# Attention scores from 32-bit two-part splits in 48 and 50 rows, two heads in the two row halves of the array, in place of bf16 splits in 112 and 115 rows

## The reference

```python
x = x + attn_a(layernorm(x))      # wide heads: 32 query heads, 8 key/value heads, head size 16
x = x + scale * (layernorm(x) @ (2 * w_ffn - 1))
x = x + attn_b(layernorm(x))
x = x + scale * (layernorm(x) @ (2 * w_ffn - 1))

# attention: q, k, v = x @ w_qkv; rope on q and k; four query heads share one key/value head
scores = einsum('bhsd,bhtd->bhst', q, k) / 4
probs = softmax(where(causal, scores, -inf))
out = einsum('bhst,bhtd->bhsd', probs, v) @ w_o
```

## Time and profile before

| | |
|---|---|
| median of three runs | 1555.02 us |
| span of the profiled execution | 1552.2 us, mean granted clock 0.979 |
| PE busy | 1439.5 us, 93% (10,756 matmuls) |
| PE weight loads busy | 799.7 us, 52% |
| DVE busy | 1132.0 us, 73% |
| ACT busy | 998.2 us, 64% |
| POOL busy | 413.6 us, 27% |
| chain that ended last | PE 73%, DVE 11%, issue 8%, POOL 3%, ACT 3%, DMA 1% |

### The profile page before, as it was taken

One profiled execution on the slowest core, in us unless ns is written; L12 is line 12 of the kernel. 1 busy time (PEld: TensorE's weight loads), 2 busy tenths in 40 slices (PEclk: granted clock), 3 DMA queues, 4 the chain that ended last, 5 costly groups with the idle time before them and its releaser, 6 DMA issues.

```text
span 1552.2 us, 36760 instructions
## 1 busy us (share of the span) xinstructions
PE 1439.5 (93%) x10756; PEld 799.7 (52%) x10756; DVE 1132.0 (73%) x1620; ACT 998.2 (64%) x1800; POOL 413.6 (27%) x786
## 2 busy tenths in 40 slices
PE   5989999998798999999879899999988899999997
PEld 4844444446674444444667444444466744444455
DVE  6897777736788777773768877777377887777646
ACT  4967667663496667675349667766625966776652
POOL 3423222212242322221224222222123422222211
PEclk9999999999899999999989999999998999999999
DMA  3000000001000000000210000000010000000001
GB/s 112 2 29 3 1 1 1 1 1 42 3 1 29 2 1 1 1 1 1 83 69 1 29 3 1 1 1 1 2 41 3 1 30 2 1 1 1 1 21 75
DMA packets 11421, 23.26 MB, mean 15 GB/s; under 512 B 816, under 2 KB 2608, under 8 KB 11312
## 3 DMA queue, kind: packets, MB, share of 16 engines
q1 hardware_dynamic: 11312, 21.89, 4.0%
HBM read 16.91 MB, written 4.19 MB: 14 GB/s over the span
## 4 chain that ended last, share of the span: by engine, by line
PE 73%; DVE 11%; issue 8%; POOL 3%; ACT 3%; DMA 1%; DVEq 0%; POOLq 0%; ACTq 0%; SPq 0%
PE psE L571 17%; PE psO L589 17%; PE psM L549 14%; PE psM L483 13%; DVE mx L974 4%; PE psM L551 3%; PE psT L466 2%; PE psT L532 2%; PE psO L532 2%; ACT probs L793 1%; PE psT L559 1%; DVE stats L876 1%; PE psE L466 1%; PE psM L466 1%; DVE xn L896 1%
## 5 line engine op out<-in xcount | busy, mean ns | idle before, releaser
L974 DVE TENSOR_REDUCE mx<-psM 128x1 f32<-128x768 f32 (+6 forms) x704 | 697.2, 1023 | 189.7 <-PE psM L551 186.7
L793 ACT ACTIVATE probs<-psE 128x512 f32<-128x512 f32 (+1 forms) x1216 | 656.8, 574 | 272.3 <-PE psE L571 261.0
L571 PE MATMUL psE<-qT,kT 115*128 (+4 forms) x1536 | 415.7, 331 | 10.5 <-ACT probs L793 7.4
L549 PE MATMUL psM<-kT,qT 112*128 (+4 forms) x1536 | 376.4, 327 | 17.9 <-DVE mx L974 13.8
L1163 POOL TENSOR_SCALAR_AFFINE_SELECT probs<-probs 128x512 f32<-128x512 f32 x256 | 162.3, 636 | 660.7 <-ACT probs L793 659.9
L589 PE MATMUL psO<-probs,v_grp 128*32 128x512 f32 (+3 forms) x3072 | 323.0, 499 | 6.3 <-POOL probs L1163 3.8
L571 PEld LDWEIGHTS psE<-qT,kT 115*128 (+1 forms) x1536 | 126.2, 97 | 289.0 <-ACT probs L793 152.5
L551 PE MATMUL psM<-tri_b,ident_b 128*128 128x128 bf16 x1024 | 210.3, 220 | 0.0
L549 PEld LDWEIGHTS psM<-kT,qT 112*128 (+1 forms) x1536 | 139.4, 98 | 108.6 <-DVE mx L974 31.1
L551 PEld LDWEIGHTS psM<-tri_b,ident_b 128*128 128x128 bf16 x1024 | 99.7, 97 | 65.5 <-issue 0.6
L589 PEld LDWEIGHTS psO<-probs,v_grp 128*32 128x32 f32 x3072 | 63.3, 108 | 104.3 <-issue 66.7
(11 more groups left out here) (90 smaller groups left out, 1553.8 us busy)
## 6 DMA issues: line engine op xcount, KB each, us to landing
probs<-in_w_qkv SPq DMA_DIRECT2D x5, 1536.0 KB, 6.3
xs<-in_x SPq DMA_DIRECT2D x8, 512.0 KB, 3.8
attn<-in_w_o SPq DMA_DIRECT2D x4, 1024.0 KB, 5.0
out_x<-xs SPq DMA_DIRECT2D x8, 512.0 KB, 3.0
qT<-nm_rows SPq DMA_DIRECT2D x64, 12.0 KB
probs<-in_w_ffn SPq DMA_DIRECT2D x1, 256.0 KB, 8.1
cos_s<-in_cos SPq DMA_DIRECT2D x1, 128.0 KB, 8.1
sin_s<-in_sin SPq DMA_DIRECT2D x1, 128.0 KB, 8.0
```

What stands on the lines that cost most here:

```text
L549: ins = pe.matmul(banks[:, at + k0:at + k1], qT[0:MAXROW, g * REP + h, qt * P:(qt + 1) * P], kT[0:MAXROW, g, k0:k1], start=True, stop=not ...
L571: ins = pe.matmul(psE[:, n % 2, at * w:(at + 1) * w], kT[0:DEPTH, g, kb * P:(kb + 1) * P], qT[0:DEPTH, g * REP + j, q0:q0 + w], start=True ...
L793: act.activation(probs[:, s % PSLOTS, heads[0]:heads[0] + len(heads), 0:w], psE[:, n % 2, 0:w * len(heads)].rearrange("p (h q) -> p h q", ...
L974: dve.tensor_reduce(mx[:, qt, heads[0]:heads[0] + len(heads)], src, AX.X, ALU.max).then_inc(unit_used.sem, 1)
```

## The change

The scores are made of two parts instead of three. Each q and k value is split into a rounded 32-bit part and its remainder (F32R). A head has 4 slots of 16 values, three of them for products of parts (48 rows) and one with two rows for the negative maximum (50 rows). Two heads share the 128 partitions of `qT`: heads 0 and 2 of a group lie in rows 0 to 63, heads 1 and 3 in rows 64 to 127, and `kT` holds the keys twice. So a product of scores uses one row half of the array. The mask is two bf16 products of 64 columns in the same half. In U a unit of several heads puts the two halves in the two banks of a pair; a unit of one head puts half of its keys in each bank.

The split is now one step on ACT (`part_h`, 1024 + 512 elements) and one on POOL (`part_l`, 512 + 256 elements); `part_m` and DVE's `part_l` are gone. PE turns a tile with 24 transposes in 32 bits, in six banks of 512 columns (ACT copies four, DVE two). The lag of R falls from 3 to 2 and the slots are written anew. The maxima are negated by the reduction itself, split in two on POOL in two instructions, turned by one transpose, and moved by two DMAs. Steps of 256 and 128 columns now take heads [0,2] and [1,3] together, so that the 128-column steps have two exponentials instead of one. `wo_hi` lies in `wq_hi`, and WQ comes later in `TAIL_ORDER`. PE's loop over the six middle groups is unrolled.

```diff
 def head_batches(step):
-    per = max(1, QCHUNK // step[3])
-    return [list(range(h, min(REP, h + per))) for h in range(0, REP, per)]
+    return [[0], [1], [2], [3]] if 2 * step[3] > QCHUNK else [[0, 2], [1, 3]]
...
-S.3.0 PV.1
+S.3.0 S.3.1 PV.1
...
-S.11.0 PV.9 O.0.0 U.21 PV.10 PV.11
+S.11.0 S.11.1 PV.9 O.0.0 U.21 PV.10 PV.11
...
 TAIL_ORDER = """
-DP.0 O.1.0 DP.1 CT.4 CT.5 CP.4 CT.6 WQ.0 CP.5 LS.2 CT.7 LR.2 WQ.1 T.2 CP.6 LM.2 T.3 LN.2 H.2
-WQ.2 CP.7 H.3 LS.3 WQ.3 LR.3 T.4 DP.2 LM.3 T.5 H.4 LN.3 DP.3 H.5 LS.4 DP.4 T.6 H.6 LR.4 DP.5
+DP.0 O.1.0 DP.1 CT.4 CT.5 CP.4 CT.6 CP.5 LS.2 CT.7 LR.2 T.2 CP.6 LM.2 T.3 LN.2 H.2
+CP.7 H.3 LS.3 LR.3 T.4 DP.2 LM.3 WQ.0 T.5 H.4 LN.3 WQ.1 DP.3 H.5 WQ.2 LS.4 DP.4 T.6 H.6 LR.4 WQ.3 DP.5
...
-LAG = {"TX": -1, "Q": 0, "R": 3, "U": 4, "HI": -1, "LO": -1, "QC": 0, "COS": 1, "ROPE": 1, "PH": 1, "PM": 2, "PL": 2,
-       "RC": 3, "ST": -4, "RS": -3, "AP": -2}
-PE_SLOT = "R.0 TX U.0 R.1 Q.0 U.1 R.2 U.2 R.3 Q.1 Q.2 R.4 U.3 Q.3"
-ACT_SLOT = "HI RC.1 PM RC.2 RS RC.3 PH QC"
-DVE_SLOT = "AP RC.0 U.0 COS LO U.1 ROPE U.2 PL RC.4 ST U.3"
+LAG = {"TX": -1, "Q": 0, "R": 2, "U": 3, "HI": -1, "LO": -1, "QC": 0, "COS": 1, "ROPE": 1, "PH": 1,
+       "RC": 2, "ST": -4, "RS": -3, "AP": -2}
+PE_SLOT = "TX U.0 Q.0 R.0 R.1 U.1 Q.1 R.2 U.2 R.3 Q.2 R.4 U.3 R.5 Q.3"
+ACT_SLOT = "HI RC.1 RC.2 RS PH RC.4 RC.5 QC"
+DVE_SLOT = "AP COS U.0 RC.0 LO ROPE U.1 RC.3 U.2 ST U.3"
...
+        wo_hi = wq_hi[:, :, 0:DIM]
-        wo_hi = sb("wo_hi", [P, KC, DIM], F32R)
...
-        qT = sb("qT", [P, HEADS, SEQ], BF16)
-        kT = sb("kT", [P, KV, SEQ], BF16)
+        qT = sb("qT", [P, KV, CHUNKS, REP // 2, QCHUNK], F32R)
+        kT = sb("kT", [P, KV, SEQ], F32R)
...
+                    def score(h, bank, at, k0, k1):
+                        lo = h % 2 * ROW
+                        pe.matmul(psM[:, 2 * pair + bank, at:at + k1 - k0],
+                                  qT[lo:lo + MAXROW, g, qt // QT_PER_CHUNK, h // 2, qt % QT_PER_CHUNK * P:(qt % QT_PER_CHUNK + 1) * P],
+                                  kT[lo:lo + MAXROW, g, k0:k1], start=True, stop=k1 < keys)
+                    def hide(h, bank, at):
+                        lo = h % 2 * ROW
+                        for half in range(2):
+                            k0 = at + half * (P // 2)
+                            ins = pe.matmul(psM[:, 2 * pair + bank, k0:k0 + P // 2], late_b[lo:lo + ROW, half, :],
+                                            half_b[lo:lo + ROW, :], start=False, stop=half == 1)
+                        return ins
+                    if len(heads) == 1:
+                        h, = heads
+                        score(h, 0, 0, 0, keys // 2)
+                        score(h, 1, 0, keys // 2, keys)
+                        ins = hide(h, 1, keys // 2 - P)
+                    else:
+                        for n_h, h in enumerate(heads[0::2]):
+                            for bank in range(2):
+                                score(h + bank, bank, n_h * keys, 0, keys)
+                            for bank in range(2):
+                                ins = hide(h + bank, bank, (n_h + 1) * keys - P)
...
-                    for at, j in enumerate(head_batches(STEPS[s])[i]):
-                        ins = pe.matmul(psE[:, n % 2, at * w:(at + 1) * w], kT[0:DEPTH, g, kb * P:(kb + 1) * P],
-                                        qT[0:DEPTH, g * REP + j, q0:q0 + w], start=True, stop=True)
+                    for n_j, j in enumerate(head_batches(STEPS[s])[i]):
+                        lo = j % 2 * ROW
+                        ins = pe.matmul(psE[:, n % 2, n_j * w:(n_j + 1) * w], kT[lo:lo + DEPTH, g, kb * P:(kb + 1) * P],
+                                        qT[lo:lo + DEPTH, g, c, j // 2, q0 - c * QCHUNK:q0 - c * QCHUNK + w], start=True, stop=True)
...
-                for n in range(1, TILES + 2):
-                    if 0 <= n - 2 < TILES:
-                        rest(n - 2, n % 2)
-                    if n - 1 < TILES:
-                        rope_sin(n - 1, (n - 1) % 2)
+                for n in range(0, TILES + 1):
+                    if n < TILES:
+                        rope_sin(n, n % 2)
+                    if 0 <= n - 1 < TILES:
+                        part_l(n - 1, (n - 1) % 2)
```

More of the change, by code:

```diff
@@ L35 @@
 PSLOTS = 3
[L42 to L45, removed]
+PARTS = 4
+ROW = PARTS * HD
+MAXROW = (PARTS - 1) * HD
+DEPTH = MAXROW + 2
+RECS = 2
+QUADS = 6
+QUAD_ACT = [1, 2, 4, 5]
+QUAD_DVE = [0, 3]
 AHEAD = TILES // 2
@@ L237, with build @@
 LS_LINKS, LM_LINKS = 2, 4
-NM_LINKS = 4
-def build(nc, x, w_qkv, w_o, w_ffn, scale, cos, sin, eye, tri, out):
+NM_LINKS = 1
+def build(nc, x, w_qkv, w_o, w_ffn, scale, cos, sin, eye, mask, out):
     with ExitStack() as ctx:
@@ L403, in load_consts @@
                 sp.dma_start(scale_s[:], scale.rearrange("(a b) -> a b", a=1).to_broadcast([P, 1])).then_inc(consts_in, 16)
-                sp.dma_start(rows[:, 0:P], tri).then_inc(consts_in, 16)
+                sp.dma_start(rows[:, 0:2 * P + P // 2], mask).then_inc(consts_in, 16)
             def put_nm(r, g, c):
                 sp.wait_ge(nm_copied.sem, nm_copied.after((r * KV + g) * CHUNKS + c))
[L409 to L412, removed]
+                n = REP * QT_PER_CHUNK
+                for a in range(2):
+                    row, at = a * ROW + MAXROW, (2 * c + a) * n
+                    sp.dma_start(
+                        qT[row:row + 2, bass.ds(g, 1), c, :, :].rearrange("p g j n -> p (g j n)").bitcast(F32),
+                        nm_rows[at:at + n, :].bitcast(F32),
+                    ).then_inc(nm_in[c], 16)
             def layers(b):
@@ L542, in unit @@
                     pe.wait_ge(unit_used.sem, unit_used.after(M - 2 if pair == n % 2 and (n == 0 or unit_pair(first, n - 1) != pair) else M - 1))
[L543 to L548, removed]
-                            ins = pe.matmul(banks[:, at + k0:at + k1], qT[0:MAXROW, g * REP + h, qt * P:(qt + 1) * P],
-                                            kT[0:MAXROW, g, k0:k1], start=True, stop=not diag)
-                        ins = pe.matmul(banks[:, at + keys - P:at + keys], ident_b[:], tri_b[:], start=False, stop=True)
+                    if first and (qt, heads[0]) == (QT_PER_CHUNK + 1, 0):
+                        pe.wait_ge(qkv_used.sem, qkv_used.after(r * TILES + TILES - 1))
@@ L557, in nm_turn @@
                     pe.wait_ge(nm_split.sem, nm_split.after(n))
[L558 to L561 removed]
+                    pe.transpose(nm_ps, nm_parts[:, c, :], ident[:]).then_inc(nm_turned.sem, 1)
                 def scores(g, s, i):
@@ L596, in o_turn @@
                     pe.wait_ge(o_copied.sem, o_copied.after(n))
-                    turn(o_T[:, c, :], psT[:], o_turned)
+                    turn(o_T[c], psT[:], o_turned)
                 def turn_c(t, k):
@@ L726, in wq_split @@
                     act.wait_ge(wq_in, n * 16 + 16)
+                    if not isinstance(n, int):
+                        act.wait_ge(projected.sem, projected.after((n - 1) * TURNS + c_turn(TILES - 1)))
                 act.activation(wq_hi[:, c, :], wq_raw[:, c, :], ACT.Copy).then_inc(wq_hi_done, 1)
@@ L774, in round_ @@
                             rec_copy(t, arg[0])
-                        elif what == "PM":
-                            part_m(t, t % 2)
                         elif what == "PH":
@@ L1016, in round_ @@
                             rope(t, t % 2)
-                        elif what == "PL":
-                            part_l(t, t % 2)
                         elif what == "ST":
@@ L1229 @@
     cos, sin = tables()
-    tri = np.where(np.arange(P)[None, :] > np.arange(P)[:, None], np.float32(-1e30), np.float32(0)).astype(np.float32)
+    late = np.where(np.arange(P)[:, None] > np.arange(P)[None, :], np.float32(-1e30), np.float32(0))
+    half = np.eye(P // 2)
+    mask = np.tile(np.concatenate([late[0:P // 2], late[P // 2:], half], 1), (2, 1)).astype(np.float32)
     arrays = {
@@ L1239 @@
         "eye": np.eye(P, dtype=np.float32),
-        "tri": tri,
+        "mask": mask,
     }
```

189 lines of the change are left out of this document (93 added, 96 removed).

## The result

| | before | after |
|---|---|---|
| median of four runs | 1555.59 us (1553.38 to 1556.79) | **2165.45 us** (2139.53 to 2202.67) |
| span of the profiled execution | 1552.2 us | 2161.7 us |
| mean granted clock of TensorE | 0.979 | **0.703** |

The changed kernel is 610 us slower by the medians. The ratio is 1.387 [1.379, 1.395]; it leaves out the one run of 2202.67 us, which fell in a slower state (granted clock 0.685). The forecast was 1599 us, with a range of 1505 to 1690. The sign was right, the size was not.

A forecast was written before the change was run, and what follows sets the result against it. The prediction took PE's stream to bound the groups and phase A: 1552.2 + 76 (phase A) - 32 (groups) = 1596 us for the profiled span, 1599 us for the median. The range was 1505 to 1690.

The forecast's parts named there:

- The step that failed: Groups, PE: a 32-bit product costs the same as bf16 at 512 columns, twice as much at 128; fewer rows shorten nothing.
- Group's period: A steady group falls from 30.9 to 29.9 us, -1.0 each and -32 in all; wrong under 28.5 or above 32.
- Overlap of the halves: Groups, PE: two heads in opposite row halves overlap like PV's column quarters, loads included.
- the third rival: Groups: halves' loads go one after another, +1.7 us each, 1685 us, 12%; products not overlapping either, +4.1, 1762 us, 6%.
- S: Score products in a group: pairs of opposite halves save 1.6 us, narrow and unpaired ones lose 0.8; together -0.8.
- ACT's cost: Groups: two more exps for the 128-column steps cost nothing while PE is the bound, otherwise some 0.2 us each.
- visits: Groups, PE: three to four more full-height transposes (N and O) standing between half-height products, +0.5 us a group.
- Phase A: Each slot goes once round a loop through POOL's rope_sin and part_l: 11.6 us against 8.0; +19 us a round, +76 in all.
- The rest of phase A and the tail: Tail: WQ moves behind H.2 and POOL's splits shift by 5 to 8 us; 0, within 2 us a round.
- The unrolled loop: PE's loop over the middle groups, unrolled: costs or gains nothing.
- The faster one: Halves overlap everywhere, S and U with masks halve until DVE takes over: -4 us a group, 1503 us; 18%.
- The one with a hidden loop through POOL: Phase A stays PE-bound at about 9 us a slot: -12 instead of +76, 1511 us; 12%.

The follow-up runs named there:

- POOL's new order: The changed kernel with POOL's part_l of tile n-1 put ahead of rope_sin of tile n; 2010.05 us (one run).

## Why the prediction was right or wrong

The 610 us come apart by the runs, each step one edit or one group of edits:

| step | us |
|---|---|
| changed kernel to POOL's new order | -155 |
| 48 and 50 rows to 64 | -303 |
| from there to the kernel before, unrolled | -175 |
| the loop rolled again | +22 |

(Each against the runs named above; the medians of the kernel before beside them differ by up to 2 us, so the steps add up to 611. Taken the other way round, 64 rows first and POOL's order second, the first two steps are -345 and -114, so the two do not simply add.)

**The step that failed** is the price of a product in the part on the groups: "one 32-bit product costs as much as a bf16 one at 512 columns", with "the depth of 48 to 50 rows instead of 112 to 115 shortens nothing". It shortens nothing (80 rows in the kernel before: 30.86 us a middle group, as with 112 to 115), and it brings the clock down: the middle groups run at 0.50 to 0.97 instead of 1.00, and 64 rows in place of 48 and 50 give back 303 us, or 345 with POOL's order as the change has it. The prediction took every duration at the upper level, from rows at 1.00, and thought of the clock only behind an idle wait in phase A. No row of the trace before shows S or U in fewer rows, so the price had no bound on the other side; a bound at the lower level (the S and U rows doubled) was what the range lacked. PV's 32-column quarters, the nearest rows for overlap, use all 128 rows and could not show this. **Group's period**: forecast 29.9 us, wrong if above 32; it was 32.1 to 33.0 at a clock of 0.97 to 0.98, and up to 50.6. The clock is the largest part of the miss and not all of it: at 64 rows with the change's own order on POOL the time is 1820.75 us, still 222 above the forecast, some 73 of them in the 28 group periods and the rest before, between and after the groups.

**Overlap of the halves: right.** Starts side by side, mask products narrow, loads of both halves in parallel (two S loads are over in 0.19 us together at 952.16); and U, sized at +0.3 - 1.0, went from 10.24 to 10.19 us with its masks. These sums are of distances from one PE start to the next, put down to the first of the two, for one group of the unrolled kernel before and of the halves of 64 rows. Both cases of the third rival, loads one after another and no overlap at all, are refuted.

**S: wrong in sign.** Forecast -0.8, by the same sums 9.07 to 11.12 us: +2.05 (+1.5 against the looped kernel before, 9.62). Two things were missed. Behind nearly every PV stands an S, and its 32-bit load is not hidden there: a lone S between two PVs takes 0.43 us (1085.45 above) where the unrolled bf16 kernel needs 0.32. And ACT: its exponentials are now 5.7% of the group's chain (1072.53 above), because the loads of S wait for the banks that ACT has to empty. The waits of the halves of 64 rows (us in total, times, longest):

```profile
PEld psE L611 <- ACT probs L825: 259.7, 503, 1.7
```

Against 390 waits of 229.9 us in the unrolled kernel before (below). How the 2.05 us divide between the two was not measured. The prediction set ACT's cost at nothing as long as PE is the bound. With the transposes of the maxima it was right in the main (0.64 to 0.52, forecast -0.2; O went from 0.93 to 1.16, a part of the forecast's "visits"). POOL's shorter chain, put at nothing, is worth 0.16 us a group in the kernel before. Together the group is 32.24 us, +2.1 against the unrolled and +1.4 against the looped kernel before, instead of -1.0.

**Phase A: right in mechanism, too small.** From Q.3's end to R.0 it took 5.6 for 5.3 us, and PE's idle time in it 3.1 to 3.4 for 3. But PE's part from R.0 took 7.75 us (596.25 to 604.00) where the forecast has 6.3, as the clock is at its lower level for a while after each wait (0.62 in the window above), a case that was only in the bounds ("+35 if PE's idle 3 us in each slot bring the granted clock down to its lower level"). In the second round slots 3 to 7 take 72.9 us together (Q.3 at 575.84 and at 648.73), where 60.3 were forecast. The ramp behind Q.3(7) was to take 18.6 us to the first S and took 30.9 in the third round (1160.25 to 1191.14): the granted clock is 0.55 there, and four transposes take 1.04 us instead of 0.44. The order on POOL alone is 28 us a round at the upper level, and 39 as the change stands; 19 was forecast for the whole of phase A against the kernel before, where the stretches grew by 60.

**The rest of phase A and the tail: "0" was wrong.** Even with POOL's new order and 64 rows, the stretch from PV.0 of the last group is 23 us longer than in the unrolled kernel before: 6 to 12 us in the last group itself, 11 to 13 from there to the last projection of phase A, up to 5 in the ramp. Of the 11 to 13, some 9 lie in the slots (64.6 us from the first Q.3 to the eighth against 55.1, in the second round), most of them at a granted clock of 1.00, so that part lies in the new slots themselves and not in the clock; the other 2 to 4 are the tail's, which was to stay within 2. In the last group the clock is 0.77 to 0.92 against 1.00, and in the ramp 0.65 to 0.84 against 1.00. How much of these two is waits and how much clock was not taken apart, and no run takes the new slots apart.

**The unrolled loop: "nothing" was wrong.** It gives -22 us, 18 of them in the 28 groups (858.9 to 841.0). Waits of the kernel before, and then of the unrolled one:

```profile
PEld psE L571 <- ACT probs L793: 152.5, 244, 1.2
PEld psE L571 <- issue: 103.5, 247, 1.7
```

```profile
PEld psE L571 <- ACT probs L793: 229.9, 390, 1.2
PEld psE L571 <- issue: 14.0, 54, 1.6
```

In the kernel before, the loads of S come late 247 times with no releaser that the profile shows; in the unrolled kernel 54 times, and there PE gets to the banks earlier and waits for ACT instead. That row ("issue", 103.5 us) stood in the trace before, and the prediction did not read it.

**Rivals.** That the clock falls for the products' height was none of them. The faster one (overlap everywhere) fell because S and U did not halve: U with its masks stayed at 10.2 us a group, and S grew, by its loads and ACT's waits. The one with a hidden loop through POOL fell by the chain.

## What to carry to other kernels

Before an edit that changes how many rows of the array a long stretch of products uses, ask what the granted clock will be, and price the stretch at both levels; look at the clock's line of the page first when the result comes. If fewer rows are wanted for the overlap of two halves, fill up each half with rows that add nothing: here that gave back 303 us, though the kernel stayed slower than the one before. And take a bundle of edits apart even when the whole is a loss: the unrolled loop alone makes the kernel before 1.5% faster.

## What the runs showed of the hardware

- The granted clock depends on how many rows the products use, not only on PE's being busy. Groups with S and U in 112/115 rows 1.00; 80 rows 1.00 after a first group at 0.94 to 0.96; 66 rows 1.00 after a first group at 0.60 to 0.95; two halves of 64 rows 1.00 with single dips to 0.69; 48/50 rows in one bf16 stream 0.50 to 0.59; 48/50 rows in halves 0.50 to 0.98. The rows added for the halves of 64 do no work for the scores, and count. Between 50 and 64 rows nothing was run.
- With PV and the masks as they are, S or U at full height alone brings most groups to 1.00. Phase A's full-height products come up again behind each wait: 0.62, then 0.88 in the windows above.
- Two row halves run side by side: 50.6 against 63.9 us a group at a clock of 0.50.
- A PE program in a loop costs 0.72 us more in each group of some 240 products than the same one unrolled (30.87 and 30.15 us).
